# Attention on one Trainium2 core: the tanh of two neighbouring ring places in one ScalarE instruction

## The reference

```
f = jnp.einsum('bih,ha->bia', x, W1[:h])
g = jnp.einsum('bjh,ha->bja', x, W1[h:])
t = jnp.tanh(f[:, :, None, :] + g[:, None, :, :] + b1)
scores = jnp.einsum('bija,a->bij', t, w2[:, 0]) + b2[0]
flag = jnp.tril(jnp.ones((n_seq, n_seq), dtype=x.dtype), -1)[None, :, :]
e = jnp.exp(scores) * flag
denom = jnp.sum(e, axis=-1, keepdims=True) + 1e-10
w = e / denom
return jnp.einsum('bij,bjh->bih', w, x)
```

## Time and profile before

| | |
|---|---|
| median of 3 runs | 7243.35 us (7242.75 to 7247.08) |
| profiled execution, span | 7243.9 us |
| attention stage | about 3145 to 7130 us of the span |
| VectorE busy over the span | 5782.1 us (80%) |
| TensorE (matmul) busy | 5755.7 us (79%) |
| ScalarE busy | 5315.5 us (73%) |
| GpSimd busy | 1440.4 us (20%) |

### The profile page before, as it was taken

The page is one execution under the profiler, slowest core; times in us unless marked ns, Lnnn a source line. Parts: engine busy times, 40 slices in busy tenths (PEclk is TensorE's granted clock), DMA queues, the critical chain, the costliest instruction groups (busy, mean ns, idle before and its releaser), DMA issues. The chain is left out here.

```text
span 7243.9 us, 89393 instructions
## 1 busy us (share of the span) xinstructions
PE 5755.7 (79%) x32962; PEld 2037.9 (28%) x32962; DVE 5782.1 (80%) x12358; ACT 5315.5 (73%) x3820; POOL 1440.4 (20%) x1695
## 2 busy tenths in 40 slices
PE   7888886788769998977777777887778887778887
PEld 3222222344324443422111222222222222222223
DVE  7888887676557775888787789989889998889996
ACT  3332322455545553579999999999999999999996
POOL 3444451000136654620000000000000000000002
PEclk8888887888869998989999999999999999999998
DMA  3111100100000000000000000000000000000000
GB/s 123 50 48 43 53 19 11 30 24 24 12 9 1 1 1 4 1 7 1 1 1 1 1 1 1 1 1 1 12 1 1 1 1 12 1 1 1 1 1 24
DMA packets 45167, 95.26 MB, mean 13 GB/s; under 512 B 7863, under 2 KB 9657, under 8 KB 43578
## 3 DMA queue, kind: packets, MB, share of 16 engines
q1 hardware_dynamic: 43834, 88.44, 3.7%
q0 software_dynamic: 896, 1.06, 0.1%
HBM read 39.14 MB, written 33.55 MB: 10 GB/s over the span
## 5 line engine op out<-in xcount | busy, mean ns | idle before, releaser
L2825 ACT ACTIVATE aa_tanh<-aa_tanh 128x4096 f32<-128x4096 f32 (+5 forms) x1120 | 3677.2, 3382 | 31.4 <-DVE aa_tanh L3005 31.1
L3005 DVE TENSOR_SCALAR aa_tanh<-aa_f_times,aa_g_bias 128x1024 f32<-128x1024 f32 (+18 forms) x5120 | 2981.3, 643 | 450.3 <-PE aa_scores L2871 443.9
L2871 PE MATMUL aa_scores<-aa_tanh,aa_w_spread 128*32 128x512 f32 (+8 forms) x18432 | 2159.9, 582 | 776.3 <-ACT aa_tanh L2825 756.5
L2871 PEld LDWEIGHTS aa_scores<-aa_tanh,aa_w_spread 128*32 128x32 f32 x18432 | 579.7, 112 | 2195.5 <-ACT aa_tanh L2825 1089.1
L2885 PE MATMUL aa_out_sum<-aa_weights,aa_normed 128*128 128x512 f32 (+3 forms) x1152 | 641.0, 640 | 67.2 <-DVE aa_weights L3014 59.7
L2793 POOL TENSOR_SCALAR aa_group_normed<-x_rows,norm_scale,aa_shift_plus 128x128 f32<-128x128 f32 x96 | 93.4, 983 | 2391.9 <-PE aa_turned L2912 1744.2
L860 PE MATMUL near_weights_spread<-near_tap_weights,near_spread_consts 36*64 36x512 f32 x3200 | 429.5, 648 | 64.7 <-DVE near_weighted L507 53.2
L2086 PE MATMUL qa_out<-qa_hidden_rows,qa_weights_in 128*128 128x512 f32 x1024 | 475.9, 608 | 0.0
L880 PE MATMUL near_out_sum<-near_weighted,near_w_out 128*128 128x512 f32 x576 | 359.1, 756 | 103.4 <-DVE near_weighted L507 103.4
L496 DVE TENSOR_TENSOR near_weights_spread<-near_weights_spread,near_values 128x1024 f32<-128x1024 f32 x256 | 313.9, 1226 | 123.9 <-PE near_weights_spread L860 122.9
L427 POOL TENSOR_TENSOR near_tap_weights<-near_hat_y_mask,near_hat_x 128x1024 f32<-128x1024 f32 x144 | 339.8, 2371 | 279.1 <-PE near_weights_spread L860 220.1
(11 more groups left out here) (433 smaller groups left out, 6777.4 us busy)
## 6 DMA issues: line engine op xcount, KB each, us to landing
near_offsets<-near_offset_staged SPq DMA_DIRECT2D x45, 512.0 KB, 3.0
l_taps<-l_scan_in_out SPq DMA_DIRECT2D x256, 64.0 KB, 2.0
x_rows<-in_x SPq DMA_DIRECT2D x4, 2048.0 KB, 15.7
near_offset_y<-near_offsets SPq DMA_DIRECT2D x15, 512.0 KB, 4.0
near_offset_x<-near_offsets SPq DMA_DIRECT2D x15, 512.0 KB
near_mask<-near_offsets SPq DMA_DIRECT2D x15, 512.0 KB, 5.3
out_x<-x_rows SPq DMA_DIRECT2D x3, 2048.0 KB, 6.3
out_x<-x_rows SPq DMA_DIRECT2D x8, 256.0 KB, 2.0
```

The lines of the kernel that those rows point to most:

```text
L2825: a.activation(TH[:, u % PLACES, 0:length], TH[:, u % PLACES, 0:length], ACT.Tanh).then_inc(th_ready, 1)
L2871: last = t.matmul(sp_[32 * q:32 * q + 32, n % 2, s:e], W2S[:, tt, :], TH[:, p, o + s:o + e], start=tt == 0, stop=tt == 3, tile_position=(0 ...
L3005: ins = v.tensor_scalar(TH[:, p, at[q]:at[q] + w - s], FR[:, m % 2, lo + s:CHUNK], GB[:, key:key + 1], None, ALU.add)
```

## The change

`two_at_once(u)` says whether place u lies in slot 0 or 2 and both u and u + 1 are full. Then ScalarE waits for the sums of both places, takes one tanh over the two neighbouring slots (128x8192) and raises `th_ready` by two; place u + 1 issues no tanh of its own. Slot 4, diagonal tiles and full places without a full partner go as before. The exponentials behind place u follow the tanh of both.

```
@@ -2700,6 +2700,14 @@
+        def is_full(u):
+
+            return u < len(places) and not shape(places[u][0])[2]
+
+        def two_at_once(u):
+
+            return u % PLACES in (0, 2) and is_full(u) and is_full(u + 1)
+
@@ -2821,8 +2829,13 @@
             for u, (n, some) in enumerate(places):
                 m, j, diagonal, lo, w = shape(n)
                 length = len(some) * runs_at(w, diagonal)[1]
-                a.wait_ge(sum_ready, 1 + u + 1)
-                a.activation(TH[:, u % PLACES, 0:length], TH[:, u % PLACES, 0:length], ACT.Tanh).then_inc(th_ready, 1)
+                if two_at_once(u):
+                    a.wait_ge(sum_ready, 1 + u + 2)
+                    pair = TH[:, u % PLACES:u % PLACES + 2, :]
+                    a.activation(pair, pair, ACT.Tanh).then_inc(th_ready, 2)
+                elif not (u and two_at_once(u - 1)):
+                    a.wait_ge(sum_ready, 1 + u + 1)
+                    a.activation(TH[:, u % PLACES, 0:length], TH[:, u % PLACES, 0:length], ACT.Tanh).then_inc(th_ready, 1)
```

## The result

| | before | changed |
|---|---|---|
| median | 7245.22 us (4 runs) | 7290.27 us (4 runs) |
| ratio | 1 | 1.0063 (1.0050 to 1.0076) |
| profiled execution | 7243.9 us | 7289.7 us |

A forecast was written before the change was run, and what follows sets the result against it. ScalarE was taken to bound the attention stage. A saving of 25.8 us against 18 (output pieces), 4 (other bursts) and 12 + 12 (TensorE's half clock) gave +20 us on 7243.9, so 7264 us, range 7222 to 7305.

The forecast's parts named there:

- Rival 3: Expert-stage pairs: two fills with expert sums outlast a round, 1 us lost in each of some 50 pairs; 7314 us, chance 0.12.
- Rival 4: ScalarE's wide tanh: the 8192 elements run as two passes and save nothing, stalls unchanged; 7290 us, chance 0.03.
- The saving: ScalarE's tanh in attention: 272 pairs each save 0.095 us, 25.8 us in all.
- Waits for sums: ScalarE waiting for VectorE to fill places: up from 31 to about 75 us, longest near last chunks' output pieces.
- The worked place: Last chunk of a batch, fill at 4733.78 us: starts 2.5 us later, and ScalarE loses 3.1 us.
- The output's pieces: VectorE adding each query chunk's output in two 4.6 us pieces behind the next chunk's first tiles: 18 us lost.
- The clock: TensorE at half clock after gathered idle time, 1.55 us a burst: 12 us near output pieces, 12 us in expert stages.
- the expert stretches: Attention stages with expert work: about a third of 24 groups lose 1.55 us at half clock, 12 us in all.
- the sentence that costs the exponentials at nothing: Exponential behind a pair's first place runs 3.5 us later; TensorE needs it only after the pair's scores, so no cost.
- The first paragraph: Opening on what bounds the kernel: ScalarE bounds attention, and its 31 us of waits for sums are almost all it lost.
- Rival 1: VectorE's reserve covers the lost fill nearly everywhere and the saving comes through: 7217.6 us, up to 7228; chance 0.2.
- rival 2: TensorE keeps its clock because each pair is a denser burst, stalls remain: -4 us, 7239.5 us, no change; chance 0.25.

The follow-up runs named there:

- e10: Changed kernel without the arithmetic of the attention output's two pieces (normalizing and adding to rows): 7229.58 us, ratio 0.9982 to the kernel before.
- e11: Kernel before the change, without the same arithmetic of the attention output's two pieces: 7202.44 us, ratio 0.9945 to the kernel before.
- e6: Kernel before the change, with extra zero-weight matmuls on TensorE, 4 of 512 columns behind each full place in passes 0 to 2: 7248.01 us, ratio 1.0005.

## Why the prediction was right

The forecast was slower, 7264 us in a range of 7222 to 7305; it came out at 7290. The sign was right, and so was the mechanism in the main: the semaphores of a pair cut VectorE's lead, and that costs more than the instruction saves. The size was less than half (20 us of 45), and part of what came out right is luck. The text gave "slower" a chance of only 0.44, and the top of its range stood on rivals 3 and 4, neither of which came true as written.

- **The saving** (25.8 us): right. The spacing of pairs is 6.92 to 6.93 us, forecast 6.92, and 0.092 us are saved a pair, forecast 0.095. (The forecast's 0.095 is a small difference of rounded times: each 0.01 us in a spacing moves it by a third.) Rival 4 (two passes) named 7290 us, just what was measured, but the spacing rules it out: the time agrees by chance.
- **Waits for sums** (31 to about 75 us): 78.8 us. The worked place lost 1.60 and 2.05 us, 3.65 together, where 3.1 were worked out, and the fill moved by 3.3 us instead of 2.5; the slow burst (0.9 us) makes up the difference. The sum fits better than its parts: of the 46 us that the forecast added, 24 stood on the clock.
- **The output's pieces** (18 us): 18 us by the medians of e10 and e11, give or take 17, and 23 us by the stretches. Right within that. That the pieces cost the kernel before 42 us, most of it in other chunks, was not seen.
- **The clock** (12 + 12 us): not shown. The granted clock fell to 0.91, not to 0.88. In the worked place it took 0.9 us, not 1.55. Filling TensorE brought the clock back in part and no time, though with a cost of its own. The time that I booked on it in the expert stretches is there, but the batch without experts had the lower clock and lost least. The Trainium skill (TensorE: Matmul & The Clock Gate, section HAM oscillation) tells of a kernel in which every burst of matmuls began at half rate, behind waits for DMA that were longer than the bursts. Here the stage's granted clock of 0.91 and a burst at 0.67 say that only part of the bursts did.
- **What was mis-sized** is the sentence that costs the exponentials at nothing, and that the gates' small exponential is not named at all. Both wait for what the late release holds up: 12.3 and 6.1 us more, each within several us. With the lost overlap of instructions that start from a wait, an estimate of 6 us, that is about the missing 25 us. I had followed the need of TensorE for the exponential, and not the need of the exponential for TensorE's scores. The rows could have warned me. The first paragraph says that 31 us of waits for sums are almost all that ScalarE lost; but by the earlier trace rows it was idle for 69.5 us, and the view of its waits, shown above, gives the exponentials 38.1 us, more than the sums, and the gates 10.8.
- **Rivals.** Rival 1 (the lead holds) fell to the waits for sums, rival 2 (stalls without the clock, no change) to the time, and to a clock that fell from 0.95 to 0.91. Rival 3 had part of the truth: the expert stretches lose most, but as many short waits (39 before pairs, the longest 2.5 us), 8 to 13 us a batch more than the first and not 50 us in all.

## What to carry to other kernels

Before you merge two steps of a ring, work out the lead and not the idle time: 443.9 us of idle VectorE did not pay for one fill of lead, because the idle time came where nothing was short. A merged step wants its inputs sooner and returns its buffers later, and the two together cost more than each alone (here 64 us against -4 and 27). Follow every instruction on the waiting engine, the small ones too: each has a releaser that the late return can move. And read all that the bounding engine waits for, not only the wait that the change touches.

## What the runs showed of the hardware that was not expected

A tanh of 128x8192 on ScalarE has the same cost per element as one of 128x4096, with one start less: the spacing is 6.92 us against 2 x 3.51 us, so the second 4096 elements add 3.42 us, 0.83 ns each, the slope that the prediction took from 2880 to 4096 elements. TensorE's granted clock over the span went down to 0.897 in a kernel whose only change was a ring of four (e4), where TensorE was idle for 962 us of 3955 instead of 922; raising it from 0.95 to 0.98 in the attention by matmuls with zero weights (e6) left the time unchanged within 0.15%.
